# GNN node pass on one core: where the bias of the node product is added

## The chip, the cores and the metric

The kernel runs on one core of a Trainium2 chip. The metric is the device time of one execution in microseconds, the median over runs. A core has five engines that run their own instruction streams and meet at semaphores: TensorE (PE, matrix products into the accumulators), VectorE (DVE), ScalarE (ACT), GpSimd (POOL) and SyncE (SP, which here issues DMAs).

## The reference, cut to what matters

Four graph layers follow each other over 50000 nodes of 128 features and 25000 edges. After each one the input is added and every row is normalised. The change concerns the third layer's end and what is computed from it for the fourth:

```
x2   = output of the second layer, normalised            # 50000 x 128
agg  = edge terms of layer 3, summed per node             # 50000 x 128, from the pass before
sfeat = (x2 @ W + b) / (in_deg + 1)
x3   = layernorm(x2 + agg(+ b) + sfeat)
xt   = x3 @ W4.T + bias4                                  # layer 4's transform
alpha_src, alpha_dst = per-head sums of xt * a_src, xt * a_dst
```

Here b appears twice, once plainly and once divided by in_deg + 1. With rin = 1 / (in_deg + 1), a node's row before normalising is x2 + agg + b + rin * (x2 @ W + b).

## The kernel before

All phases run one after the other in one launch. Most of the time goes to layer 2, whose gathers are issued by GpSimd. The phase of interest is the combined node pass, which computes x3 and xt in one sweep. The nodes lie in 30 chunks (CHUNKS), each of 128 partitions by 13 columns (NJ) by 128 features, and a tail of 80 rows. Three slots (SLOTS) of buffers rotate.

For a chunk c in slot s the work goes through these steps. The semaphore that ends each step is in brackets.

- SP loads x2 into X2L and agg into YL (`load`, d_ld). It does so when the same slot's normalised rows have been stored (`store`).
- GpSimd, in `add` (lines 1927 to 1941): it copies the chunk's 13 values of nsrc into R1 (line 1930), multiplies the broadcast bias B2 by the broadcast R1 into the tile BT (line 1933), adds X2L onto YL (line 1937) and adds BT onto YL (line 1941, d_x2y). nsrc was set to rin + 1 at the head of the phase by VectorE (line 1972), so BT is b * (rin + 1).
- TensorE, in `turn`: it transposes X2L in groups of four columns (line 2106, d_t); ACT copies each group out of the accumulators into HT or OT (line 2036, `turned`, d_tc); TensorE multiplies it by W into one of two accumulator banks, SUM + q % 2 (line 2116, d_z).
- VectorE, in `rows`: per group q, it waits for the product (d_z), and for each column adds rin times the product onto YL (line 2001, scalar_tensor_tensor, d_v1). Then `spread` takes the statistics of the group before (line 1989). After the four groups (4, 4, 4 and 1 columns) come the statistics of the last one and the aggregates to mean and variance (line 2011, d_st).
- GpSimd, in `scale`: (variance + eps) to the power -1/2 and minus the mean times that (lines 743 to 749, d_rdy).
- ACT normalises each column into X3 (line 2042, `applied`, d_x3).
- TensorE, in `transform`: it transposes X3 (line 2127), ACT copies (line 2053), and TensorE multiplies by the fourth layer's matrix (line 2137, d_q) in groups of three columns. VectorE, in `transformed`, adds that layer's bias into O3 (line 2019) and copies the attention part (line 2025); SP stores.

Each engine has a fixed order. GpSimd: scale(c), add(c+2), scale(c+1), and so on. VectorE and TensorE: rows or turn of c+1, then transformed or transform of c. ACT mixes: the copy of group 0 of chunk c+1, the normalising of group 0 of chunk c, the copy of group 1, the normalising of group 1, and so on, and then the transform's copies of chunk c. TensorE may overwrite an accumulator bank only when VectorE's scaled additions from it are done (d_v1).

Of the kernel before, what the change touches and what calls it, by code (L numbers as in the profile page):

```python
# [7 lines left out]
P, D = 128, 128  # L8
# [18 lines left out]
NJ = 13  # L27
CHUNKS = NC_ // NJ
SLOTS = 3
# [6 lines left out]
def build(nc, x0, src, dst, ea, ew, w0, b0, w1, b1, gamma, beta, w2, b2, we, be, coef, linw, linb, asrc, adst, out):  # L36
# [8 lines left out]
    def sem(name):  # L45

        phase.append(nc.alloc_semaphore(name=name))
        return phase[-1]
# [19 lines left out]
    with ctx:  # L68
# [622 lines left out]
        def columns(table, c):  # L691

            return table[0:TAIL, NC_:NCOL] if c is None else table[:, bass.ds(c * NJ, NJ)]
# [955 lines left out]
        at = U * CW  # L1649
# [18 lines left out]
        with nc.Block() as block:  # L1668
# [193 lines left out]
        AC = big[:, at:at + 9].rearrange("p (k b) -> p k b", k=3)  # L1862
        CF = big[:, at + 16:at + 19]
        A3 = big[:, at + 32:at + 35]
        R1 = big[:, at + 40:at + 40 + NJ]
        at += 60
        BT = big[:, at:at + NJ * D].rearrange("p (j f) -> p j f", f=D)
        d_w, d_p, d_m, d_ready, d_r1, d_r1b = (sem("d_" + n) for n in "w p m ready r1 r1b".split())
        d_ld, d_x2y, d_st, d_ps, d_rdy, d_x3, d_o, d_sx, d_so = (sems("dd_" + n, SLOTS) for n in (
            "ld x2y st ps rdy x3 o sx so".split()))  # L1870
        d_t, d_tc, d_z, d_v1, d_u, d_uc, d_q, d_oc = (sem("d_" + n) for n in "t tc z v1 u uc q oc".split())
        TR, UB = (HT, OT), (5, CAR)
        QA, QB = -(-NJ // 4), -(-NJ // 3)

# [9 lines left out]
        with nc.Block() as block:  # L1884
# [38 lines left out]
            @block.gpsimd  # L1923
            def _(pool):
                pool.wait_ge(d_ready, 1)

                def add(c, s, n):
                    np_, nj = size(c)
                    y, b = YL[s][0:np_, 0:nj, :], BT[0:np_, 0:nj, :]
                    nc.gpsimd.tensor_copy(R1[0:np_, 0:nj], columns(nsrc, c)).then_inc(d_r1, 1)  # L1930
                    steady(pool, SLOTS * n + s + 1)
                    pool.wait_ge(d_r1, SLOTS * n + s + 1)
                    nc.gpsimd.tensor_tensor(b, wide(B2, np_, nj), R1[0:np_, 0:nj].unsqueeze(2)
                                            .to_broadcast([np_, nj, D]), ALU.mult).then_inc(d_r1b, 1)
                    steady(pool, 32 * n + 32)
                    pool.wait_ge(d_ld[s], 32 * n + 32)
                    nc.gpsimd.tensor_tensor(y, y, X2L[s][0:np_, 0:nj, 0:D], ALU.add).then_inc(d_x2y[s], 1)
                    steady(pool, SLOTS * n + s + 1, 2 * n + 1)
                    pool.wait_ge(d_r1b, SLOTS * n + s + 1)
                    pool.wait_ge(d_x2y[s], 2 * n + 1)  # L1940
                    nc.gpsimd.tensor_tensor(y, y, b, ALU.add).then_inc(d_x2y[s], 1)

                def scale(c, s, n):
                    ln_scale(pool, c, s, n, d_st, d_ps, d_rdy)
                add(0, 0, 0)
                add(1, 1, 0)
                with pool.Fori(0, CHUNKS // SLOTS - 1) as i:
                    for u in range(SLOTS):
                        scale(SLOTS * i + u, u, i)
                        add(SLOTS * i + u + 2, (u + 2) % SLOTS, i + (u + 2) // SLOTS)  # L1950
                m = CHUNKS // SLOTS - 1
                scale(CHUNKS - 3, 0, m)
                add(CHUNKS - 1, 2, m)
                scale(CHUNKS - 2, 1, m)
                add(None, 0, m + 1)
                scale(CHUNKS - 1, 2, m)
                scale(None, 0, m + 1)

            @block.vector
            def _(dve):  # L1960
# [8 lines left out]
                                                                    ALU.mult, ALU.add))  # L1969
                nc.vector.tensor_scalar(B3C, ones[:], A3[:, 2:3], None, ALU.mult)  # L1970
                nc.vector.tensor_copy(IDA[:, 0:D], ident[:])
                nc.vector.tensor_scalar(nsrc[:], rin[:], 1.0, None, ALU.add)
                link(dve, "dve", nc.vector.memset(IDA[:, D:DX], 0.0))
                for k in range(2):
                    for q in range(HEADS):
# [16 lines left out]
                def rows(c, s, n):  # L1992

                    np_, nj = size(c)
                    steady(dve, 2 * n + 2)
                    dve.wait_ge(d_x2y[s], 2 * n + 2)
                    for q, js in groups(c, 4):
                        dve.wait_ge(d_z, before_chunk(c, QA) + q + 1)
                        for j in js:
                            rc = rin[0:np_, NC_:NCOL] if c is None else rin[:, bass.ds(c * NJ + j, 1)]  # L2000
                            ins = nc.vector.scalar_tensor_tensor(YL[s][0:np_, j, :], PS[0:np_, SUM + q % 2, j % 4, :],
                                                                 rc, YL[s][0:np_, j, :], ALU.mult, ALU.add)
                        ins.then_inc(d_v1, 1)
                        if q:
                            spread(c, s, q - 1, groups(c, 4)[q - 1][1])
                    q, js = groups(c, 4)[-1]
                    spread(c, s, q, js).then_inc(d_st[s], 1)
                    steady(dve, 2 * n + 1)
                    dve.wait_ge(d_st[s], 2 * n + 1)
                    for j in range(nj):  # L2010
                        ins = nc.vector.bn_aggr(mv[0:np_, s, j, :], st6[0:np_, j, :])
                    ins.then_inc(d_st[s], 1)
# [415 lines left out]
```

## Time and profile before

| | |
|---|---|
| median of 3 runs | 9455.91 us (9445.86 to 9458.88) |
| profiled execution | 9455.72 us, span 9453.9 us |
| mean granted TensorE clock | 0.63 |
| GpSimd busy | 6665.9 us (71%) |
| TensorE busy | 5807.2 us (61%) |
| VectorE busy | 4952.6 us (52%) |
| ScalarE busy | 2449.6 us (26%) |

The busy shares are means over phases with different limits. The node pass lies between about 7938 and 8392 us from the span's start, so only what the views show of this stretch bears on the change. In the rows, L numbers are lines of the kernel before; a name such as big stands for many tiles that are cut out of one large buffer (X2L, YL, X3, O3, BT among them), and PS stands for the accumulators.

### The profile page before, as it was taken

The page shows a single profiled execution, that of the slowest core. Times are in us where ns is not written, and L with a number is a line of the kernel's source. Part 1 is how long each engine was busy: PE and PEld are TensorE (multiplying, and loading weights), DVE is VectorE, ACT ScalarE, POOL GpSimd, SP SyncE. Part 2 cuts the span into 40 slices and gives each one's busy share as a digit, 9 for nine tenths or more (in the row PEclk, how much of TensorE's full clock was granted, in tenths as well). Part 3 has the DMA queues.
Part 4 walks back from the last instruction along what each step waited for, and adds up shares of the span by engine and source line. Part 5 has one row for each costly group of instructions (what it writes and reads, how often), then busy time and mean ns, then how long its engine had stood idle before and what let it go on. Part 6 is the DMA issues. An engine that isn't in the chain of part 4 may idle for free. (4 is left out here: it accounts for less than half of the span.)

```text
span 9453.9 us, 109668 instructions
## 1 busy us (share of the span) xinstructions
PE 5807.2 (61%) x24229; PEld 4281.7 (45%) x24229; DVE 4952.6 (52%) x12073; ACT 2449.6 (26%) x6228; POOL 6665.9 (71%) x6509
## 2 busy tenths in 40 slices
PE   4646556777775677765777765777751676730190
PEld 2436223555554555554555544555541565630170
DVE  5669665563334753335743345633347675630277
ACT  0116000222224222224222233222236112630006
POOL 4767674477777777777777777777777677977566
PEclk8765786775555765555855556855555787975555
DMA  3127101566664766654766666666656223631118
GB/s 146 43 89 264 29 2 26 110 119 100 101 104 98 129 111 99 101 100 103 137 102 101 101 100 115 124 101 105 101 100 226 83 67 119 248 125 29 20 32 330
DMA packets 472142, 1025.40 MB, mean 108 GB/s; under 512 B 146139, under 2 KB 179724, under 8 KB 471396
## 3 DMA queue, kind: packets, MB, share of 16 engines
q0 software_dynamic: 192032, 330.70, 29.6%
q1 hardware_dynamic: 262212, 589.56, 17.4%
q10 hardware_dynamic: 17664, 102.61, 2.6%
q8 instruction: 75, 1.23, 0.1%
q14 instruction: 159, 1.30, 0.0%
HBM read 562.28 MB, written 472.47 MB: 109 GB/s over the span
## 5 line engine op out<-in xcount | busy, mean ns | idle before, releaser
L1018 POOL DMA_INDIRECT G<-tab,gidx x4000 | 3960.3, 990 | 1617.0 <-issue 1408.4
L1365 PE MATMUL PS<-M,G 128*128 128x128 f32 x6400 | 2257.8, 476 | 1299.6 <-DMA G<-tab,gidx 902.2
L1365 PEld LDWEIGHTS PS<-M,G 128*128 128x128 f32 x6400 | 1549.4, 311 | 2032.7 <-DMA G<-tab,gidx 1451.9
L1313 ACT ACTIVATE M<-ident,wz 128x128 f32<-128x128 f32 x3200 | 1021.5, 390 | 2376.5 <-DVE UO L1421 1223.8
L1421 DVE TENSOR_TENSOR_SCAN UO<-keyrow,UT,PS 128x512 f32<-128x512 f32 (+1 forms) x400 | 511.8, 1279 | 1290.5 <-PE PS L1365 1290.5
L1421 DVE TENSOR_TENSOR_SCAN UT<-keyrow,UO,PS 128x512 f32<-128x512 f32 (+1 forms) x400 | 511.8, 1279 | 1190.4 <-PE PS L1365 1190.4
L758 ACT ACTIVATE big<-big,nb,rs 128x128 f32<-128x128 f32 x1173 | 461.3, 480 | 426.7 <-POOL nb L749 360.3
L1105 POOL DMA_INDIRECT Y<-pair_d,G x400 | 402.7, 1007 | 199.8 <-issue 130.6
L1443 DVE TENSOR_TENSOR Y<-PS,big 128x512 f32<-128x512 f32 x800 | 535.9, 670 | 14.0 <-PE PS L1390 7.5
L1390 PE MATMUL PS<-ident,UT 128*128 128x128 f32 x1600 | 422.5, 419 | 8.3 <-DVE UT L1421 8.3
L1390 PE MATMUL PS<-ident,UO 128*128 128x128 f32 x1600 | 423.1, 420 | 0.0
L1368 PE MATMUL PS<-ident,G 128*128 128x128 f32 x800 | 189.2, 308 | 358.3 <-DMA G<-tab,gidx 308.0
L1331 ACT ACTIVATE M<-PS,tcol,scol 128x512 f32<-128x512 f32 x200 | 155.5, 778 | 842.2 <-PE PS L1368 842.2
L1257 PE MATMUL PS<-big 128*128 128x400 f32 x800 | 323.6, 531 | 43.2 <-DVE G L1151 25.9
L1390 PEld LDWEIGHTS PS<-ident,UT 128*128 128x128 f32 x1600 | 343.0, 228 | 14.7 <-DVE UT L1421 14.7
L1390 PEld LDWEIGHTS PS<-ident,UO 128*128 128x128 f32 x1600 | 346.1, 229 | 0.0
L2270 PE MATMUL PS<-ident,cf 128*100 128x128 f32 x8 | 2.0, 426 | 517.4 <-DVE cf L2216 517.4
L450 POOL DMA_INDIRECT G<-in_x,ridx x200 | 207.6, 1038 | 157.5 <-DVE ridx L520 95.1
L2314 POOL DMA_INDIRECT agg<-Y,sidx x200 | 197.8, 989 | 153.5 <-DVE Y L2365 105.0
L902 POOL DMA_INDIRECT gidx<-lastpos,src_i x200 | 229.9, 1149 | 102.4 <-issue 67.3
L1368 PEld LDWEIGHTS PS<-ident,G 128*128 128x128 f32 x800 | 108.8, 148 | 418.9 <-DMA G<-tab,gidx 366.3
L1384 PE MATMUL PS<-cf 128*128 128x512 f32 x400 | 261.0, 741 | 14.6 <-DVE UT L1421 7.6
(500 smaller groups left out, 11173.4 us busy)
## 6 DMA issues: line engine op xcount, KB each, us to landing
tab<-Y SPq DMA_DIRECT2D x1050, 256.0 KB, 2.8
big<-agg SPq DMA_DIRECT2D x90, 832.0 KB, 8.2
G<-tab,gidx POOLq DMA_INDIRECT x4000, 3.8
WR<-w_d SPq DMA_DIRECT2D x200, 256.0 KB
big<-x SPq DMA_DIRECT2D x60, 832.0 KB, 4.9
xt_d<-big SPq DMA_DIRECT2D x30, 884.0 KB, 3.6
x2n<-big ACTq DMA_DIRECT2D x30, 838.5 KB, 3.5
big<-x2n SPq DMA_DIRECT2D x30, 838.5 KB, 5.4
```

What stands on the lines that cost most here:

```text
L758: ins = nc.scalar.activation(X[0:np_, j, 0:D], V[0:np_, j, :], ACT.Identity, scale=rs[0:np_, s, j:j + 1], bias=nb[0:np_, s, j:j + 1])
L902: pool.indirect_dma_start(gidx[:, t:t + 1], None, lastpos, bass.IndirectOffsetOnAxis(ap=src_i[:, t:t + 1], axis=0)).then_inc(g_got, 16)
L1018: pool.indirect_dma_start(G[:, t % RG, 0:D], None, tab_in(k), bass.IndirectOffsetOnAxis(ap=gidx[:, t:t + 1], axis=0)).then_inc(l_got[t % R ...
L1105: pool.indirect_dma_start(GS[:, t, :], None, pair_d, bass.IndirectOffsetOnAxis(ap=G2[:, t:t + 1], axis=0)).then_inc(o_got, 16)
L1257: ins = nc.tensor.matmul(bank2(n % 2)[:, j, :], OH[:, 2 * n + j, :], CT, start=True, stop=True)
L1313: ins = nc.scalar.activation(M[:, GR * h + j, :], ident[:], ACT.Copy, scale=wz[:, bass.ds((NB * i + q) * GR + j, 1)])
L1365: ins = nc.tensor.matmul(PS[:, FT_[h], j, :], G[:, s, 0:D], M[:, GR * h + j, :], start=True, stop=True)
L1368: ins = nc.tensor.transpose(PS[:, FT_[h], j, :], G[:, s, 0:D], ident[:])
L1384: nc.tensor.matmul(bank(BK_[h]), QR[:, q % NG, :], BD, start=True, stop=False)
L1390: ins = nc.tensor.transpose(PS[:, BK_[h], j, :], UR[h][:, j, :], ident[:])
L1421: nc.vector.tensor_tensor_scan(S[h], keyrow[:, bass.ds(tile * P, GR * P)], half if k == 0 else bank(FT_[h]), S[1 - h][:, GR * P - 1:GR * P ...
L1443: nc.vector.tensor_tensor(group_of(Y, q % NG), PS[:, BK_[h], :, :], zt_at((NB * i + q) * GR).rearrange("p (s f) -> p s f", f=D), ALU.add). ...
```

## The change

VectorE now adds the broadcast bias to a group's product in the accumulator bank, in place, in one instruction per group of up to four columns, and signals it on a new semaphore d_zb. The scaled additions of the group wait for it; they then add rin * (product + b). The statistics of the group before move to between the bias addition and the wait, so they now come ahead of the group's scaled additions and not behind them. GpSimd no longer copies the column and no longer multiplies; its second addition adds the broadcast bias itself. The column R1, the tile BT, their two semaphores and VectorE's setup instruction for nsrc are gone.

```diff
-                    y, b = YL[s][0:np_, 0:nj, :], BT[0:np_, 0:nj, :]
-                    nc.gpsimd.tensor_copy(R1[0:np_, 0:nj], columns(nsrc, c)).then_inc(d_r1, 1)
-                    steady(pool, SLOTS * n + s + 1)
-                    pool.wait_ge(d_r1, SLOTS * n + s + 1)
-                    nc.gpsimd.tensor_tensor(b, wide(B2, np_, nj), R1[0:np_, 0:nj].unsqueeze(2)
-                                            .to_broadcast([np_, nj, D]), ALU.mult).then_inc(d_r1b, 1)
+                    y = YL[s][0:np_, 0:nj, :]
                     steady(pool, 32 * n + 32)
                     pool.wait_ge(d_ld[s], 32 * n + 32)
                     nc.gpsimd.tensor_tensor(y, y, X2L[s][0:np_, 0:nj, 0:D], ALU.add).then_inc(d_x2y[s], 1)
-                    steady(pool, SLOTS * n + s + 1, 2 * n + 1)
-                    pool.wait_ge(d_r1b, SLOTS * n + s + 1)
+                    steady(pool, 2 * n + 1)
                     pool.wait_ge(d_x2y[s], 2 * n + 1)
-                    nc.gpsimd.tensor_tensor(y, y, b, ALU.add).then_inc(d_x2y[s], 1)
+                    nc.gpsimd.tensor_tensor(y, y, wide(B2, np_, nj), ALU.add).then_inc(d_x2y[s], 1)
...
-                nc.vector.tensor_scalar(nsrc[:], rin[:], 1.0, None, ALU.add)
...
                     for q, js in groups(c, 4):
                         dve.wait_ge(d_z, before_chunk(c, QA) + q + 1)
+                        product = PS[0:np_, SUM + q % 2, 0:len(js), :]
+                        nc.vector.tensor_tensor(product, product, wide(B2, np_, len(js)), ALU.add).then_inc(d_zb, 1)
+                        if q:
+                            spread(c, s, q - 1, groups(c, 4)[q - 1][1])
+                        dve.wait_ge(d_zb, before_chunk(c, QA) + q + 1)
                         for j in js:
                             rc = rin[0:np_, NC_:NCOL] if c is None else rin[:, bass.ds(c * NJ + j, 1)]
                             ins = nc.vector.scalar_tensor_tensor(YL[s][0:np_, j, :], PS[0:np_, SUM + q % 2, j % 4, :],
                                                                  rc, YL[s][0:np_, j, :], ALU.mult, ALU.add)
                         ins.then_inc(d_v1, 1)
-                        if q:
-                            spread(c, s, q - 1, groups(c, 4)[q - 1][1])
```

## Rows read from the trace of the kernel before

**Rows 1.** Windows: stretch, length, each engine's busy time (instructions), clock, DMA share, GB/s.
```profile
7983.64:8363.27 379.63, 293.60 (x2107) 249.62 (x2108) 261.18 (x1215) 240.52 (x595) 362.32 (x216) 0.99 0.63 244
8363.27:8376.62 13.35, 10.10 (x73) 8.32 (x72) 9.67 (x45) 8.55 (x22) 4.42 (x7) 1.00 0.34 135
```

**Rows 2.** Groups by line, 7965 to 8370: busy us, mean ns, then idle before.
```profile
L1941 POOL TENSOR_TENSOR big<-big 128x1664 f32<-128x1664 f32 (+1 forms) x30 | 108.4, 3613 | 5.1 <-POOL big L1937 5.1
...
L1937 POOL TENSOR_TENSOR big<-big 128x1664 f32<-128x1664 f32 (+1 forms) x29 | 96.0, 3311 | 0.0
L1933 POOL TENSOR_TENSOR big<-big 128x1664 f32<-128x1664 f32 (+1 forms) x29 | 84.4, 2910 | 4.2 <-POOL big L1930 0.2
...
L746 POOL TENSOR_TENSOR rs<-rs,minus_half 128x13 f32<-128x13 f32 x29 | 71.2, 2457 | 2.4
```

**Rows 3.** Timeline of an early chunk: start, us, engine, line, count, [idle before, releaser].
```profile
7979.80 1.04 DVE L2019 TENSOR_TENSOR big<-PS,big 128x408 f32<-128x408 f32 x2
7980.04 0.27 POOL L743 TENSOR_SCALAR rs<-mv 128x13 f32<-128x13 f32 x1 [0.37 <-DVE mv L2011]
...
7983.14 0.59 ACT L2036 COPY HT<-PS 128x512 f32<-128x512 f32 x1 [1.30 <-PE PS L2106]
...
7983.64 1.65 ACT L2042 ACTIVATE big<-big,nb,rs 128x128 f32<-128x128 f32 x4
...
7985.08 1.13 DVE L2001 SCALAR_TENSOR_TENSOR big<-PS,rin,big 128x128 f32<-128x128 f32 x4 [1.78 <-PE PS L2116]
7985.20 0.56 ACT L2036 COPY OT<-PS 128x512 f32<-128x512 f32 x1
...
7985.81 1.16 PE L2116 MATMUL PS<-big,OT 128*128 128x128 f32 x8 [0.44 <-ACT OT L2036]
...
7987.12 1.13 DVE L2001 SCALAR_TENSOR_TENSOR big<-PS,rin,big 128x128 f32<-128x128 f32 x4 [0.91 <-PE PS L2116]
...
7989.14 1.13 DVE L2001 SCALAR_TENSOR_TENSOR big<-PS,rin,big 128x128 f32<-128x128 f32 x4
...
7990.18 0.86 DVE L1989 BATCH_NORM_STATS2 st<-big 128x6 f32<-128x128 f32 x4
...
7990.96 0.33 DVE L2001 SCALAR_TENSOR_TENSOR big<-PS,rin,big 128x128 f32<-128x128 f32 x1
...
7992.37 0.97 DVE L2011 BATCH_NORM_AGGREGATE mv<-st 128x2 f32<-128x6 f32 x13
...
7993.26 1.04 DVE L2019 TENSOR_TENSOR big<-PS,big 128x408 f32<-128x408 f32 x2
```

**Rows 4.** Timeline: VectorE reads accumulators in another phase.
```profile
2013.52 0.67 DVE L1426 TENSOR_TENSOR big<-PS,bias 128x512 f32<-128x512 f32 x1
2014.10 0.68 DVE L1443 TENSOR_TENSOR Y<-PS,big 128x512 f32<-128x512 f32 x1
```

**Rows 5.** Groups of VectorE by form, whole run.
```profile
L1421 DVE TENSOR_TENSOR_SCAN UO<-keyrow,UT,PS 128x512 f32<-128x512 f32 x320 | 409.5, 1280 | 929.4 <-PE PS L1365 929.4
...
L342 DVE MEMSET PS<- 128x4096 f32 x1 | 3.5, 3472 | 0.9 <-DVE wccol L341 0.9
```

**Rows 6.** Timeline of the tail's one group on VectorE.
```profile
8376.62 0.35 DVE L2001 SCALAR_TENSOR_TENSOR big<-PS,rin,big 80x128 f32<-80x128 f32 x1 [0.33 <-PE PS L2116]
...
8377.01 0.29 DVE L1989 BATCH_NORM_STATS2 st<-big 80x6 f32<-80x128 f32 x1
8377.40 0.18 DVE L2011 BATCH_NORM_AGGREGATE mv<-st 80x2 f32<-80x6 f32 x1
```

**Rows 7.** Timeline of the pass's start.
```profile
7955.26 2.16 DVE L2001 SCALAR_TENSOR_TENSOR big<-PS,rin,big 128x128 f32<-128x128 f32 x8 [10.84 <-POOL big L1941]
...
7965.62 0.28 POOL L743 TENSOR_SCALAR rs<-mv 128x13 f32<-128x13 f32 x1
...
7969.26 1.65 ACT L2042 ACTIVATE big<-big,nb,rs 128x128 f32<-128x128 f32 x4 [8.78 <-POOL nb L749]
```

**Rows 8.** Waits, 7965 to 8370: us in total, times, longest.
```profile
DVE big L2001 <- PE PS L2116: 97.8, 60, 6.6
```

More of the change, by code:

```diff
@@ L1864, in build @@
         A3 = big[:, at + 32:at + 35]
-        R1 = big[:, at + 40:at + 40 + NJ]
         at += 60
-        BT = big[:, at:at + NJ * D].rearrange("p (j f) -> p j f", f=D)
-        d_w, d_p, d_m, d_ready, d_r1, d_r1b = (sem("d_" + n) for n in "w p m ready r1 r1b".split())
+        d_w, d_p, d_m, d_ready = (sem("d_" + n) for n in "w p m ready".split())
         d_ld, d_x2y, d_st, d_ps, d_rdy, d_x3, d_o, d_sx, d_so = (sems("dd_" + n, SLOTS) for n in (
             "ld x2y st ps rdy x3 o sx so".split()))
-        d_t, d_tc, d_z, d_v1, d_u, d_uc, d_q, d_oc = (sem("d_" + n) for n in "t tc z v1 u uc q oc".split())
+        d_t, d_tc, d_z, d_zb, d_v1, d_u, d_uc, d_q, d_oc = (sem("d_" + n) for n in "t tc z zb v1 u uc q oc".split())
         TR, UB = (HT, OT), (5, CAR)
```

## The prediction

> **What bounds the kernel now.** I read the page first (shares and the slices), then the windows of the node pass, its groups of instructions, its waits, and last the timeline of one chunk. Over the whole run GpSimd is the busiest engine, but most of that is gather issue in other phases. The change is inside the combined node pass alone, some 450 us of the 9454, in 30 chunks of 13 columns and a tail. So the question is what one chunk costs there.
>
> Call a round the time from one chunk's first normalising activation (ACT L2042) to the next chunk's. From chunk 1 to chunk 28 there are 27 rounds in 379.63 us, so 14.06 us each, and GpSimd is busy for 362.32 of them, 13.4 a round [rows 1]. The groups say with what: three passes over 1664 elements, 2.91, 3.31 and 3.61 us on average, and the power for the inverse root, 2.46 [rows 2]. With its small instructions and gaps that is the whole round: GpSimd sets the pace. The TensorE clock was granted at 0.99, its upper level.
>
> But a second ring lies just below. The last full round has almost no GpSimd work (4.42 us busy) and still takes 13.35 us [rows 1]. The timeline of an early chunk shows the ring's members [rows 3]:
> - ACT copies the turned group 0 of the next chunk (7983.14), 0.50 later it starts to normalise group 0 of this chunk (7983.64), 1.56 later it copies turned group 1 (7985.20), 0.61 later TensorE multiplies it by W (7985.81), 1.31 later VectorE's scaled addition of group 1 starts (7987.12).
> - From there VectorE is back to back: group 2 starts 2.02 later (7989.14), group 3 1.82 after that (7990.96), the aggregates 1.41 after that (7992.37), and the additions of the transform 0.89 after that (7993.26).
> - From those additions to the copy of the next chunk's group 0 it is 3.34 (7979.80 to 7983.14), through TensorE's last products and its next transposes.
>
> Sum: 0.50 + 1.56 + 0.61 + 1.31 + 2.02 + 1.82 + 1.41 + 0.89 + 3.34 = 13.46 us. The other way round, through GpSimd, is as long: its scale step starts 0.24 after the transform's additions (7979.80 to 7980.04, the one place where it waited for VectorE, 0.37 us) and the activation comes 3.60 after that; 0.24 + 3.60 = 3.84, just the 3.34 + 0.50 of the other branch. So GpSimd's 14.06 stands over a ring of latencies of 13.46, only 0.6 us less.
>
> **The change part by part.**
>
> *GpSimd's bias product and column go.* Per chunk 2.91 to 3.00 us and a copy with its gap, 3.3 together. GpSimd then needs 14.06 - 3.3 = 10.8 us a round. This alone would give the round to the ring: 13.46. The remaining additions keep their number; the second now reads a broadcast instead of a filled tile. The pass that read broadcasts took 2.91, the one that read two filled tiles 3.61 [rows 2]: 0 to 0.7 us gained, no matter where the round is over 11.
>
> *VectorE adds the bias in the accumulators.* Three additions of 512 elements and one of 128 per chunk. Nothing in the trace adds from an accumulator into an accumulator. The nearest rows read an accumulator and write SBUF: 0.67 us, and the next instruction starts 0.58 later [rows 4]. Bounds from both sides: a fill of all 4096 elements of the accumulators took 3.47 us, so 0.43 for 512 of writing; and the slowest two-input 512-element form on this engine, the scan, took 1.28 [rows 5]. I take 0.60 as the start-to-start price, beside the 0.58, and 0.25 for the 128-element one, a quarter of the 1.04 that four scaled additions take (7989.14 to 7990.18).
>
> The Trainium skill prices this differently: Perfetto Trace Analysis, Optimizing Scalar/DVE Operations, gives VectorE some 125 ns of access per instruction on PSUM, which on top of 512 elements at the 0.96 GHz of VectorE: DVE Perf Modes is an estimate of 0.66 between starts. The row says 0.58; by the page the total below would be some 3 us more.
>
> *Where these stand.* Group 0 is covered. VectorE starts it 5.28 after the transform's additions (7979.80 to 7985.08) [rows 3]; with the addition (0.67), the new wait (0.1) and four scaled additions (1.04) it is done at 7.1, and group 1's product arrives at 3.34 + 3.98 = 7.32. So the idle before group 1 pays for it, with 0.2 to spare. From group 1 on it is not covered, as VectorE has no idle left in the ring:
> - group 1 to 2: 0.60 + four statistics 0.78 (7990.18 to 7990.96) + 1.04 = 2.42 in place of 2.02, so +0.40 (0.20 of the old time was a wait for TensorE, which is absorbed)
> - group 2 to 3: 2.42 in place of 1.82, +0.60
> - group 3 to the aggregates: 0.25 + 0.78 + 0.39 + 0.39 = 1.81 in place of 1.41, +0.40. The two 0.39 are new: the statistics of group 3 now stand right behind the scaled addition they read. The tail shows both steps bare: 8376.62, 8377.01, 8377.40 [rows 6]. Before, group 2's statistics hid the first.
>
> The other new wait, for the bias addition, is hidden for groups 1 to 3 by the statistics of the group before. Queued behind it on VectorE is only the scaled addition itself. TensorE waits for that one before it overwrites an accumulator; group 2's product is wanted 2.02 after group 1's and is ready by then, as the scaled addition of group 0 ends before group 1's begins.
>
> The ring is then 13.46 + 0.40 + 0.60 + 0.40 = 14.86 us, both branches alike, as they part only behind the aggregates. That is 0.80 a round *more* than the 14.06 that GpSimd imposed: the change takes 3.3 us off an engine that was 0.6 over the ring, and puts 1.4 on the ring.
>
> *Loads.* A chunk's tiles are asked for when its slot's normalised rows are stored, and GpSimd will want them some 3 us sooner than now. It has 14.86 - 10.8 = 4 us a round of slack, so even a wait of 3 us there is hidden.
>
> *Start and end.* Now the first scaled addition starts at 7955.26 and waits for GpSimd's three passes; then GpSimd does chunk 1's passes, and scales chunk 0 only at 7965.62, 3.64 before the first activation at 7969.26 [rows 7]. After: the setup loses one column instruction (0.3) and GpSimd 3.1, so VectorE starts near 7951.8. Its chunk takes 1.82 + 2.42 + 2.42 + 1.81, and 1.1 for the aggregates and the signal, 9.6 in all, to 7961.4, where GpSimd is already free. The first activation comes 4.2 earlier. The first round grows by 1.4, as does the last full one, which never waited for GpSimd. The tail's own bias addition runs under the last chunk's 13 activations and costs nothing.
>
> Sum: -4.2 + 1.4 + 27 x 0.80 + 1.4 = +20.2 us. The profiled execution lasted 9455.72 (span 9453.9), and the median shown is 9455.91, so its time stands for the median. Forecast: **9476 us**, +0.21%.
>
> **The rivals.**
> - *The additions fall into VectorE's idle time.* That idle is real: 97.8 us in 60 waits for TensorE's product [rows 8], 3.5 us a round against 2.05 added. If groups 2 and 3 came late enough from ACT and TensorE, the ring would stay at 13.46 and the round would fall by 0.6: 27 x -0.60 - 4.2 = -20, 9436 us. It decides if the idle lies behind group 1. Against it: of the idle 0.91 to 1.78 us at a time stands ahead of group 0 and of group 1 [rows 3], and only 0.2 behind. Chance 0.11.
> - *Writing accumulators is dear.* At 0.9 us start to start, groups 1 and 2 cost 0.3 each more, group 3 0.1, and group 0 outgrows its cover by 0.1: a round of 15.7, 27 x 1.6 + 2 x 2.2 - 3 = +45, 9500 us. At the scan's 1.2 it would be near 9528. For it: no row shows this form. Against it: the fill writes 512 in 0.43. Chance 0.16.
> - *Half of it is absorbed.* Between the ring and the rounds there may be slack that I took for fixed: were only 0.7 of the 1.4 to show, the round would be 14.16 and the total 27 x 0.1 - 4 + 1 = 0, 9456 us. This would happen if ACT, whose next copies follow its own queue, gave group 1 sooner. Against it: 13.35 and 13.46 in two rounds of different kinds. Chance 0.12.
> - *The forecast,* with the start-to-start price between 0.55 and 0.67 and 0.1 of error in the small steps: 9468 to 9485. Chance 0.61.
>
> **How the numbers follow.** What a measurement of this kernel can tell from no change is some 0.2%, 19 us, so slower begins at 9475, inside the forecast's own range. I split its 0.61 into 0.34 above and 0.27 below. Slower: 0.34 + 0.16 = 0.50. Same: 0.27 + 0.12 = 0.39. Faster: 0.11. The range for 8 in 10 reaches from the half-absorbed case to the dear accumulators: 9454 to 9500.
>
> **What the changed profile would show.** Right: rounds of ACT L2042 near 14.9; GpSimd busy near 10.3 a round, with idle before its scale step released by VectorE's aggregates; an idle before group 0 and group 1 only, the second near 0.2; a bias addition near 0.67 with the next start 0.6 later; the first activation near 7965. Wrong: rounds of 13.5, or idle between the bias addition of group 2 and its scaled addition; a bias addition well over 0.7 us; a GpSimd that still never waits; a TensorE clock that falls in the pass.

## The result and the profile after

The changed kernel takes 9468.03 us (median of 20 runs, 9459.94 to 9480.95), the kernel before 9450.84 in as many. The ratio is 1.0018, with a 95% interval of 1.0011 to 1.0025: slower by about 17 us. The forecast was 9476, +20.2 on its own base. Two executions of the kernels below stood far out (12583.7 us of e1_gp_alone, 10008.3 of e6_pe_bias_copies_first); they don't count in the ratios.

The profiled execution after lasted 9470.05 us, span 9468.1; the clock is as before (0.63), TensorE and ScalarE are so within 0.3%, VectorE has 64 us more, GpSimd 99 us less. In the page's first part (busy us, share, instructions):

```profile
PE 5791.9 (61%) x24229; PEld 4293.8 (45%) x24229; DVE 5016.2 (53%) x12193; ACT 2446.4 (26%) x6228; POOL 6566.6 (69%) x6447
```

Phases in which nothing was changed differ between executions: this pass begins 6.4 us earlier than in the profile before, and over all profiles below its start varies by 21 us. So below I measure the pass itself, in the one profiled execution of each kernel. VectorE writes a one-element note ahead of the pass and behind it, and the timeline of these gives the length of the pass after:

```profile
7925.40 0.06 DVE L170 MEMSET note<- 1x1 f32 x1 [16.81 <-PEq L52]
8405.29 0.06 DVE L170 MEMSET note<- 1x1 f32 x1
```

That is 479.89 us. Between the same two notes the kernel before takes 463.34 (7931.78 to 8395.12). So the pass is 16.55 longer, which accounts for the difference of the medians, 17.19. The windows of the pass after, as those of [rows 1], hold the 27 rounds and the last full one:

```profile
7973.84:8371.19 397.35, 286.34 (x2106) 245.35 (x2106) 317.53 (x1323) 237.59 (x595) 278.73 (x163) 1.00 0.60 234
8371.19:8385.84 14.65, 10.18 (x73) 8.53 (x73) 11.76 (x49) 8.54 (x24) 3.83 (x6) 1.00 0.31 123
```

A round is now 14.72 us on average in place of 14.06 and the last one 14.65 in place of 13.35. GpSimd is busy for 10.3 us of a round, no longer 13.4. The waits of the two engines within the 27 rounds (total us, count, longest) say who waits now:

```profile
POOL rs L743 <- DVE mv L2005: 101.6, 27, 4.1
...
DVE PS L1991 <- PE PS L2110: 47.1, 27, 1.9
```

GpSimd waits 3.8 us a round for VectorE's aggregates, where before all its waits for them came to 0.7 us in 27 rounds. VectorE waits 1.7 us for TensorE once a round, ahead of group 0; ahead of group 1 some 0.15 is left (below), and behind it none. The groups of instructions of the pass give the price of the new operation (lines renumbered: L1991 is the bias addition, L1997 the scaled addition):

```profile
L1991 DVE TENSOR_TENSOR PS<-PS,big 128x512 f32<-128x512 f32 x90 | 62.7, 696 | 63.8 <-PE PS L2110 55.0 <-POOL big L1933 7.5
...
L1991 DVE TENSOR_TENSOR PS<-PS,big 128x128 f32<-128x128 f32 x30 | 8.7, 290 | 0.0
```

And the timeline of one early chunk, the counterpart of [rows 3]:

```profile
7970.01 1.04 DVE L2013 TENSOR_TENSOR big<-PS,big 128x408 f32<-128x408 f32 x2
...
7970.25 0.27 POOL L743 TENSOR_SCALAR rs<-mv 128x13 f32<-128x13 f32 x1 [4.90 <-DVE mv L2005]
...
7973.35 0.58 ACT L2030 COPY HT<-PS 128x512 f32<-128x512 f32 x1 [1.30 <-PE PS L2100]
...
7973.84 1.65 ACT L2036 ACTIVATE big<-big,nb,rs 128x128 f32<-128x128 f32 x4
...
7975.18 0.70 DVE L1991 TENSOR_TENSOR PS<-PS,big 128x512 f32<-128x512 f32 x1 [1.67 <-PE PS L2110]
7975.40 0.56 ACT L2030 COPY OT<-PS 128x512 f32<-128x512 f32 x1
...
7976.01 1.16 PE L2110 MATMUL PS<-big,OT 128*128 128x128 f32 x8 [0.43 <-ACT OT L2030]
7976.02 1.13 DVE L1997 SCALAR_TENSOR_TENSOR big<-PS,rin,big 128x128 f32<-128x128 f32 x4
7977.21 0.70 DVE L1991 TENSOR_TENSOR PS<-PS,big 128x512 f32<-128x512 f32 x1
7977.81 0.86 DVE L1980 BATCH_NORM_STATS2 st<-big 128x6 f32<-128x128 f32 x4
7978.59 1.11 DVE L1997 SCALAR_TENSOR_TENSOR big<-PS,rin,big 128x128 f32<-128x128 f32 x4
7979.62 0.69 DVE L1991 TENSOR_TENSOR PS<-PS,big 128x512 f32<-128x512 f32 x1
...
7982.02 0.29 DVE L1991 TENSOR_TENSOR PS<-PS,big 128x128 f32<-128x128 f32 x1
...
7983.77 0.97 DVE L2005 BATCH_NORM_AGGREGATE mv<-st 128x2 f32<-128x6 f32 x13
7984.65 1.04 DVE L2013 TENSOR_TENSOR big<-PS,big 128x408 f32<-128x408 f32 x2
...
7988.00 0.58 ACT L2030 COPY HT<-PS 128x512 f32<-128x512 f32 x1 [1.30 <-PE PS L2100]
7988.48 1.65 ACT L2036 ACTIVATE big<-big,nb,rs 128x128 f32<-128x128 f32 x4
```

Walk the ring from 7973.35: 0.49 to the activation, 1.56 to the copy of group 1, 0.61 to its product and 1.20 to its bias addition (7977.21). VectorE then steps through 7979.62, 7982.02, 7983.77 and 7984.65, that is 2.41, 2.40, 1.75 and 0.88, and it is 3.35 to the next copy. Together 14.65. It is the ring of the prediction, with VectorE back to back from group 1's addition on. Ahead of that addition stand 1.19 us for group 0's four scaled additions (7976.02 to 7977.21), which take 1.03 where nothing is waited for (7978.59 to 7979.62): the difference, 0.16, is the wait for group 1's product.

### The profile page after: what moved, and what is told of

The parts are those of the page before. It is cut to its first block and busy times, and to the rows that moved or that the text cites. A ratio compares the mean times of both kernels' runs of the same rounds, so it can differ in the third digit from the quotient of the medians.

```text
span 9468.1 us, 109641 instructions
## 1 busy us (share of the span) xinstructions
PE 5791.9 (61%) x24229; PEld 4293.8 (45%) x24229; DVE 5016.2 (53%) x12193; ACT 2446.4 (26%) x6228; POOL 6566.6 (69%) x6447
```

## The experiments

The theory: before, GpSimd's 14.06 a round stood 0.6 over a ring of latencies of 13.46; the change takes GpSimd off the path and puts three new steps of VectorE on the ring, from group 1 on. The rivals: the work taken off GpSimd gives nothing, the additions fall into idle time, or the cost is in the moved statistics rather than in the additions. Each kernel ran 5 to 11 times beside the kernel before on the same chip. First all results; "pass" is the time between the two notes of VectorE in the profiled execution, and the kernel before has 463.34 in it. A round is from one chunk's first activation to the next one's; where two figures stand, the second, 0.23 to 0.32 longer, is every third round.

| kernel | median us | ratio to before | 95% interval | pass us | against before | round us |
|---|---|---|---|---|---|---|
| after | 9468.03 | 1.0018 | 1.0011 to 1.0025 | 479.89 | +16.55 | 14.64 / 14.88 |
| e1_gp_alone | 9423.57 | 0.9979 | 0.9970 to 0.9989 | 443.04 | -20.30 | 13.45 / 13.69 |
| e2_dve_alone | 9467.67 | 1.0028 | 1.0018 to 1.0037 | 483.87 | +20.53 | 14.65 / 14.88 |
| e3_old_order | 9503.94 | 1.0065 | 1.0051 to 1.0079 | 523.40 | +60.06 | mostly 16.0 to 16.7 |
| e4_group0_only | 9431.18 | 0.9986 | 0.9977 to 0.9995 | 443.00 | -20.34 | 13.45 / 13.69 |
| e5_pe_bias | 9448.93 | 0.9992 | 0.9983 to 1.0001 | 455.52 | -7.82 | 13.45 / 13.77 |
| e6_pe_bias_copies_first | 9452.54 | 0.9998 | 0.9989 to 1.0007 | 459.20 | -4.14 | 12.76, 13.96, 14.25 |
| e7_old_order_pe_busy | 9492.96 | 1.0043 | 1.0029 to 1.0057 | 500.29 | +36.95 | 15.31 / 15.54 |
| e8_no_power | 9471.63 | 1.0019 | 1.0009 to 1.0028 | 476.81 | +13.47 | 14.64 / 14.87 |
| e9_pe_bias_early_split | 9425.23 | 0.9983 | 0.9974 to 0.9992 | 443.67 | -19.67 | 13.45 / 13.77 |
| e10_pe_bias_copies_first_busy | 9403.89 | 0.9958 | 0.9944 to 0.9971 | 423.76 | -39.58 | 12.76 / 13.08 |
| e11_after_copies_first | 9454.21 | 1.0014 | 1.0005 to 1.0023 | 472.73 | +9.39 | 14.50 / 14.74 |

The medians of the kernel before beside them were 9442.27 (e1 to e4), 9455.21 (e5 to e8) and 9442.68 (e9 to e11). The differences of the medians agree with those of the pass to within 5 us, but for e4_group0_only: its median is 11.1 us under the kernel before and its pass 20.3. All differences of the pass lie within the 95% intervals.

**The two halves of the change.** First GpSimd's half alone, from the changed kernel (it leaves out the bias over in_deg + 1, so its result differs):

```diff
-                        nc.vector.tensor_tensor(product, product, wide(B2, np_, len(js)), ALU.add).then_inc(d_zb, 1)
-                        if q:
-                            spread(c, s, q - 1, groups(c, 4)[q - 1][1])
-                        dve.wait_ge(d_zb, before_chunk(c, QA) + q + 1)
...
+                        if q:
+                            spread(c, s, q - 1, groups(c, 4)[q - 1][1])
```

> GpSimd's part of the change alone: no column copy, no multiplication, VectorE without the bias addition and with its old order (the share of the bias divided by in_deg + 1 is left out of the result). Ring theory: GpSimd was 0.6 us a round over a ring of latencies of 13.46 us, so of its 3.3 us a round only 0.6 shows: rounds of 13.4 to 13.5, 27 x -0.6 and some -5 to -6 at the start, -20 to -22 us in all. Rival, GpSimd as the true bound of the pass: rounds of 10.8, -90 us. Rival, VectorE's waits absorb nothing and something else holds the rounds at 14: -5 us.

Measured: rounds of 13.45, the ring's length, as the timeline of ACT shows (a third round of 13.69, then one of 13.45):

```profile
8107.03 1.65 ACT L2033 ACTIVATE big<-big,nb,rs 128x128 f32<-128x128 f32 x4
...
8120.72 1.65 ACT L2033 ACTIVATE big<-big,nb,rs 128x128 f32<-128x128 f32 x4
...
8134.17 1.65 ACT L2033 ACTIVATE big<-big,nb,rs 128x128 f32<-128x128 f32 x4
```

So taking GpSimd's product away does give something, 20.30 us, of which 14.4 are in the 27 rounds and 6.1 ahead of the first activation, and no more than the ring below allows. Then VectorE's half alone, from the kernel before, with GpSimd's copy and product kept in its queue and only not read by its last addition:

```diff
-                    nc.gpsimd.tensor_tensor(y, y, b, ALU.add).then_inc(d_x2y[s], 1)
+                    nc.gpsimd.tensor_tensor(y, y, wide(B2, np_, nj), ALU.add).then_inc(d_x2y[s], 1)
...
+                        nc.vector.tensor_tensor(product, product, wide(B2, np_, len(js)), ALU.add).then_inc(d_zb, 1)
```

> VectorE's part alone: bias addition in the accumulators and the moved statistics, while GpSimd still copies the column and multiplies (its product is computed and not used; it adds the broadcast bias as in the changed kernel). Ring theory: GpSimd's 14.0 us of work fits inside a ring of 14.65, so the rounds are as long as in the changed kernel (14.7) and only the start's gain of 4.6 us is missing: +21 to +22 us against before, some 4 us above the changed kernel. Rival, the multiplication still counts a round (shared ports, or GpSimd still on the path): rounds of 15.2 or more, +35 us.

Measured: the rounds are those of the changed kernel to 0.01 us. Under a ring of 14.65 GpSimd's three passes fit, so their removal is worth nothing in a round. This pass is 3.98 us longer than the changed one's: the first activation, which follows GpSimd's first chunk, comes 4.70 later (37.57 into the pass against 32.87), and the tail is 0.82 shorter (18.63 against 19.45).

**Which additions cost.** The first half again, with the addition to group 0 alone (the share of the other groups is left out):

```diff
+                        if q == 0:
+                            product = PS[0:np_, SUM + q % 2, 0:len(js), :]
+                            nc.vector.tensor_tensor(product, product, wide(B2, np_, len(js)), ALU.add).then_inc(d_zb, 1)
+                            dve.wait_ge(d_zb, (CHUNKS if c is None else c) + 1)
```

> As the first kernel of this call, but VectorE adds the bias in the accumulators for group 0 alone (left out for groups 1 to 3), with its bare wait. Ring theory: group 0 stands in the idle ahead of group 1, so its 0.84 us a round costs nothing: the same time as GpSimd's part alone, within 2 us, about -20 against before. Rival, VectorE's time counts wherever it stands: 28 x 0.84 = +23 over GpSimd's part alone, so about +2 against before.

Measured: 443.00 in the pass against 443.04 without it. In its timeline the scaled additions of group 0 follow 0.84 behind the addition, and those of group 1 another 1.28 on:

```profile
8102.38 0.70 DVE L1992 TENSOR_TENSOR PS<-PS,big 128x512 f32<-128x512 f32 x1 [1.67 <-PE PS L2111]
8103.22 1.13 DVE L1996 SCALAR_TENSOR_TENSOR big<-PS,rin,big 128x128 f32<-128x128 f32 x4
8104.50 1.13 DVE L1996 SCALAR_TENSOR_TENSOR big<-PS,rin,big 128x128 f32<-128x128 f32 x4
```

Four of them take 1.03 from start to start (7978.59 to 7979.62 above, with no gap), so about 0.2 of the cover was left. In these two passes group 0's addition is free, and the whole cost is that of groups 1 to 3. The medians say it less sharply: this kernel's is 7.6 us above that of the first half. The added time that the rival named (+2 against before, ratio 1.0002) lies outside this kernel's interval, but no trace was kept of an execution at its median, so where the 7.6 us lie is open.

**What the moved statistics do.** The changed kernel, with the statistics back behind the scaled additions:

```diff
-                        if q:
-                            spread(c, s, q - 1, groups(c, 4)[q - 1][1])
                         dve.wait_ge(d_zb, before_chunk(c, QA) + q + 1)
...
                         ins.then_inc(d_v1, 1)
+                        if q:
+                            spread(c, s, q - 1, groups(c, 4)[q - 1][1])
```

> The changed kernel with the statistics put back behind the scaled additions, so that VectorE waits bare for each bias addition. Ring theory: bias addition 0.70 + 0.14 wait in place of 0.60 start to start, for groups 1 and 2 each +0.25, group 3 +0.09: rounds of 15.2 to 15.3, +33 us against before (+16 against the changed kernel). Rival, the wait is cheap and the order does not matter: +17 as the changed kernel.

Measured: 523.40, 43.5 more than the changed kernel and far more than a bare wait can cost (0.84 from the addition's start to its reader's, against 0.60 to an independent instruction). The timeline shows an addition's bare wait, and then something else:

```profile
8112.86 0.68 DVE L1991 TENSOR_TENSOR PS<-PS,big 128x512 f32<-128x512 f32 x1
...
8113.69 1.13 DVE L1995 SCALAR_TENSOR_TENSOR big<-PS,rin,big 128x128 f32<-128x128 f32 x4
...
8118.95 1.70 PE L2131 MATMUL PS<-big,UO 128*128 128x136 f32 x6 [2.39 <-DVE big L2013]
...
8120.65 1.53 PE L2131 MATMUL PS<-big,UT 128*128 128x136 f32 x6
```

Six products with 136 columns, 0.96 us for the same shape earlier in the chunk, take 1.70 after TensorE has stood idle for 2.39. The windows around the idle time give the granted clock in the third column from the end:

```profile
8112.90:8118.90 6.00, 3.41 (x26) 2.84 (x26) 5.61 (x32) 1.98 (x5) 1.13 (x3) 0.98 0.81 305
8118.90:8120.50 1.60, 1.55 (x7) 1.58 (x8) 0.39 (x1) 0.00 (x0) 1.52 (x2) 0.50 1.00 412
```

It fell from 0.98 to 0.50, the lower of its two levels (1.2 GHz), and those products are on the ring. To tell that from the order itself, the same kernel with products whose result nobody reads, into an accumulator that is free, ahead of the wait in which TensorE stood idle, in the chunks of the loop:

```diff
+                        if q == 2 and not isinstance(g, int):
+                            for j in range(12):
+                                nc.tensor.matmul(PS[:, PA, j % 4, :], W2, ident[:], start=True, stop=True)
```

> The kernel with the statistics in the old order (e3_old_order), and TensorE does 12 products of 128 columns into free accumulators ahead of its long wait for VectorE in the transform (their result is never read). In e3_old_order some rounds took 15.26 us, as worked out, and most 16.2 to 16.7, with TensorE's products at 1.5 to 1.7 us in place of 0.94 after 2.4 us of idle. Clock theory: TensorE without the long idle keeps its upper level, all rounds are 15.3, +33 to +37 us against before. Rival, the long rounds come from the order itself or from memory: +60 us or more, as the fillers only add work.

Measured: rounds of 15.31, the best rounds of the one before (15.26), and a granted clock of 1.00 over 300 us in place of 0.92. Windows of the two kernels, old order first:

```profile
8000.00:8300.00 300.00, 215.92 (x1434) 188.72 (x1433) 220.86 (x913) 160.33 (x400) 186.64 (x111) 0.92 0.56 218
```

```profile
8000.00:8300.00 300.00, 257.81 (x2001) 230.09 (x2000) 233.82 (x964) 169.36 (x423) 198.44 (x118) 1.00 0.59 230
```

So at least 23.1 of the 43.5 us were the clock; the last chunks, outside the loop, have no such products, and one of their rounds still takes 16.39. The rounds in the loop stay 0.66 us above the changed kernel's. The bare waits account for it by the sum made ahead of the run (+0.25, +0.25 and +0.09 for groups 1 to 3, 0.59), which no run splits further. The place of the statistics, which I had only counted as cover, saves more (43.5 us) than the additions cost in it (479.89 - 443.04 = 36.85).

**Both branches.** The changed kernel without GpSimd's power, 2.45 us of its branch of the ring. The call is replaced by its own instructions, without the power that stood between the second and the third:

```diff
-                    ln_scale(pool, c, s, n, d_st, d_ps, d_rdy)
...
+                    nc.gpsimd.tensor_scalar(rs[0:np_, s, 0:nj], mv[0:np_, s, 0:nj, 1], EPS, None, ALU.add)
+                    nc.gpsimd.tensor_scalar(nb[0:np_, s, 0:nj], mv[0:np_, s, 0:nj, 0], -1.0, None,
+                                            ALU.mult).then_inc(d_ps[s], 2)
...
+                    nc.gpsimd.tensor_tensor(nb[0:np_, s, 0:nj], nb[0:np_, s, 0:nj], rs[0:np_, s, 0:nj],
+                                            ALU.mult).then_inc(d_rdy[s], 1)
```

> The changed kernel without the power in GpSimd's scale step (the rows are scaled by variance + eps instead of its inverse root, so the result differs), 2.46 us less between the aggregates and ScalarE. By the prediction both branches of the ring are alike, through GpSimd's scale step and through the transform and the copy of group 0, and ScalarE does the copy first: rounds stay at 14.65 to 14.75, +16 to +18 us against before, the first activation 2.5 us earlier and the last one too. Rival, the ring closes through GpSimd alone: rounds of 12.2, -50 us.

Measured: the rounds stay at 14.64; only the ends lose 3.1 us. So the ring's other branch, through TensorE's transposes and ACT's copy, holds the ring by itself, and GpSimd's branch was no longer than it.

**Moving the bias to TensorE.** The first half alone leaves TensorE with idle time. Here a product of ones with the bias row, split into three bf16 parts, starts each accumulation, while TensorE waits for ACT's copy:

```diff
+                        nc.tensor.matmul(PS[0:np_, SUM + q % 2, 0:len(js), :], ONB[:, 0:np_], wide(BB, P, len(js)),
+                                         start=True, stop=False, skip_group_check=True)
+                        pe.wait_ge(d_tc, g + 1)
...
-                                                   start=True, stop=True)
+                                                   start=False, stop=True, skip_group_check=True)
```

> TensorE adds the bias: ahead of its wait for ScalarE's copy it starts each accumulator group with one single-pass bf16 product of a matrix of ones with the bias split into three bf16 rows (their sum is the fp32 bias), and the products by W accumulate onto it. VectorE has no bias addition and its old order, GpSimd no multiplication. Ring theory: four short products a chunk fall into TensorE's idle time ahead of each product (0.24 to 0.75 us), nothing is added to the ring: rounds of 13.4 to 13.5 with 13.7 in every third, -18 to -22 us against before, level with GpSimd's part alone. Rival, TensorE is the next bound and each start of a group delays the product by its own 0.2 to 0.4: rounds of 14 and more, -5 us or nothing.

Measured: the rounds are 13.45, so the bias costs a round nothing there. But the pass is 12.5 longer than the bare first half, and not level with it as expected. Of this 11.4 lie ahead of the first activation (42.71 us into the pass against 31.35), where VectorE splits the bias row, and 0.9 in the tail:

```profile
7924.31 3.38 POOL L1934 TENSOR_TENSOR big<-big 128x1664 f32<-128x1664 f32 x1 [23.36 <-DVE big L1977]
7924.47 3.31 DVE L1981 CAST big<-big 128x128 bf16<-128x128 f32 x1
...
7927.84 3.82 POOL L1937 TENSOR_TENSOR big<-big 128x1664 f32<-128x1664 f32 x1
7928.14 3.60 DVE L1983 CAST big<-big 128x128 bf16<-128x128 f32 x1
7931.77 3.37 DVE L1984 TENSOR_TENSOR big<-big 128x128 f32<-128x128 f32 x1
7935.17 3.74 DVE L1985 CAST big<-big 128x128 bf16<-128x128 f32 x1
```

Instructions on 128 elements take as long as GpSimd's additions of 1664 beside them. Its first subtraction, by chance between two of GpSimd's additions, took 0.29. The next kernel has the same split earlier, while GpSimd is still idle:

```diff
                 nc.vector.tensor_copy(col[:, 6:7], ones[:, 0:1]).then_inc(d_p, 1)
+                nc.vector.memset(ONB, 1.0)
...
+                ins.then_inc(d_bb, 1)
                 dve.wait_ge(d_m, 1)
```

> e5_pe_bias with the split of the bias into bf16 rows moved ahead of the point where GpSimd starts its additions. In e5_pe_bias the rounds were 13.45 us as worked out, but the pass was only 7.8 us shorter than before and not 20: VectorE's four instructions of the split that touch GpSimd's port each took 3.3 to 3.7 us, as long as GpSimd's addition beside them, and TensorE's first transposes waited for them. Port theory: alone on VectorE they take 0.2 to 0.3 us each, mostly inside the 1.45 us in which VectorE waits for TensorE, so the pass is 19 to 21 us shorter than before, -18 to -22 us. Rival: these instructions are slow by themselves (conversion to bf16), and the loss of 12 us stays: -8 us.

```profile
7933.39 0.16 DVE L1977 CAST big<-big 128x128 bf16<-128x128 f32 x1
7933.59 0.29 DVE L1978 TENSOR_TENSOR big<-big 128x128 f32<-128x128 f32 x1
7933.91 0.23 DVE L1979 CAST big<-big 128x128 bf16<-128x128 f32 x1
```

The same instructions take 0.16 to 0.29, the first activation comes at 31.44, the pass is 443.67, and the gain of the first half is kept with the full computation done: 0.9983.

**Shortening the ring.** ACT copies the turned groups 0 and 1 before it normalises, so that group 1's product no longer waits for four activations:

```diff
-                        if k < len(first):
-                            turned(ahead, *first[k])
+                        if k == 0:
+                            for f in first[0:2]:
+                                turned(ahead, *f)
+                        elif k + 1 < len(first):
+                            turned(ahead, *first[k + 1])
```

On top of TensorE's bias (with the late split):

> As the run before it in this call, and ScalarE copies group 1 of the next chunk ahead of the first normalising group of this one, so that the first normalising group (1.56 us) leaves the ring. Ring theory: what is left is VectorE from group 0 on, 5.28 + 1.04 + 1.04 + 0.78 + 1.04 + 0.78 + 0.25 + 1.16 + 0.89 = 12.26, and the chain over the normalised rows and the transform at 12.3 to 12.9: rounds of 12.3 to 12.9, -40 to -50 us against before. Rival, the 13.46 is set by something else than this ring (loads, TensorE): rounds stay at 13.5, -20 us.

Measured: one round in three is 12.76, as worked out, but the others are 13.96 and 14.25, and most of the gain is lost. In a long round TensorE's transposes and products come behind 1.45 us of idle time and take 1.40 and 1.73, in a short one 0.88 and 0.96; the granted clock is 0.57 over these 4 us of the long round and 1.00 over the same steps of the short one. The timeline of a long one, then of a short one:

```profile
8119.39 1.40 PE L2138 MATMUL PS<-ident,big 128*128 128x128 f32 x6 [1.45 <-ACT big L2047]
...
8120.71 1.73 PE L2148 MATMUL PS<-big,UO 128*128 128x136 f32 x6
...
8133.62 0.88 PE L2138 MATMUL PS<-ident,big 128*128 128x128 f32 x6 [1.45 <-ACT big L2047]
...
8134.74 0.96 PE L2148 MATMUL PS<-big,UO 128*128 128x136 f32 x6 [0.24 <-ACT UO L2058]
```

The same edit with the early split, and four unread products into a free accumulator ahead of the wait in which TensorE stood idle:

```diff
+                        for j in range(4):
+                            nc.tensor.matmul(PS[:, PA, j, :], W2, ident[:], start=True, stop=True)
```

> e6_pe_bias_copies_first with the early split, and with four products of 128 columns on TensorE into free accumulators (never read) ahead of its wait for the normalised rows. In e6_pe_bias_copies_first one round in three took 12.76 us, inside the 12.3 to 12.9 worked out, and two 13.96 and 14.25, with TensorE's transposes and products at 1.4 and 1.73 in place of 0.88 and 0.96 behind an idle of 1.45 us, the granted clock at 0.92 over 300 us in place of 1.00. Clock theory: with the idle filled, all rounds take 12.8, 13.0 in every third: 27 x -1.2 and -5 at the start, -35 to -42 us against before. Rival: the longer rounds come from GpSimd's waits for the loads (2 us a round): rounds of 13.5 to 14 stay, -15 us.

Measured: 12.76 and 13.08 in all rounds, 423.76 in the pass, 9403.89 us. Windows of the kernel without the products and of the one with them:

```profile
8000.00:8300.00 300.00, 261.89 (x1807) 230.06 (x1806) 213.19 (x987) 194.84 (x485) 226.34 (x130) 0.92 0.66 255
```

```profile
8000.00:8300.00 300.00, 277.52 (x2102) 243.43 (x2103) 223.18 (x1042) 205.59 (x514) 239.74 (x141) 1.00 0.70 274
```

The clock went from 0.92 to 1.00. The early split doesn't explain the rounds: without ACT's edit they were 13.45 with the late and with the early one. This version beats both kernels: 0.9958 against the kernel before (0.9944 to 0.9971), 38.8 us. And the changed kernel itself with ACT's edit alone:

> The changed kernel with ScalarE's copy of group 1 ahead of its first normalising group, and nothing else. Ring theory: the slack that the prediction gave group 0 (0.2 us) is all there is before VectorE alone sets the round: from the transform's additions 5.2 to group 0, 0.84 + 1.04 for it, then 2.41 + 2.40 + 1.75 + 0.88 = 14.5, in place of 14.65: -4 us against the changed kernel, +13 against before. If TensorE now idles longer ahead of the normalised rows its clock may fall as in e6_pe_bias_copies_first, and rounds of 15.5 to 16 stand beside them. Rival: the first normalising group is still what holds the ring, and rounds fall by its 1.56 us: 13.1, -30 us.

Measured: 14.50 in place of 14.65. With group 1's product no longer late, VectorE is back to back from group 0 on; its wait ahead of group 1 was 0.15 us, which is all that the same edit gives a round here, against 0.7 where VectorE has no additions. The pass is 7.16 shorter than the changed kernel's: 3.9 of this are in the 27 rounds, the rest at the two ends (the tail is 18.31 in place of 19.45).

## Why the prediction held

By its steps, each against the pass:

| step | predicted | measured |
|---|---|---|
| start to the first activation | -4.2 | -4.61 (37.48 to 32.87) |
| first round | +1.4 | +1.19 (14.38 to 15.57) |
| 27 rounds | +21.6 | +17.72 (379.63 to 397.35) |
| last full round | +1.4 | +1.30 (13.35 to 14.65) |
| tail | 0 | +0.95 (18.50 to 19.45) |
| sum | +20.2 | +16.55 |

- *GpSimd stands 0.6 over a ring of 13.46.* Shown by its half alone: 13.45.
- *Group 0 is covered, with 0.2 to spare.* Shown by the kernel with group 0 alone, within 0.04 us of the pass without.
- *GpSimd's removal is worth nothing under the new ring, and about 4 at the start.* Shown by VectorE's half alone: same rounds, 4.70 at the start. The other branch of the ring is no longer than the first: shown by the kernel without the power.
- *The price of an addition.* Predicted 0.60 from start to start, by the row of an addition that reads accumulators and writes SBUF [rows 4]. Measured 0.60 (7977.21 to 7977.81), and a busy time of 0.696. The Trainium skill's access time (Perfetto Trace Analysis, Optimizing Scalar/DVE Operations) made an estimate of 0.66; the measurement decides for 0.60.
- *The mis-sized term: 27 rounds at +0.80.* They cost 17.72 / 27 = 0.66 each. The ring is 14.65, not 14.86. Of this difference of 0.21, 0.11 is the step from the product's start to VectorE, now 1.20 where the scaled addition came 1.31 behind it [rows 3], and 0.10 the steps on VectorE (2.41, 2.40, 1.75, 0.88 against 2.42, 2.42, 1.81, 0.89). Most of the latter is group 3, whose two steps I took bare from the tail [rows 6]. Against that I left something out: every third round is 0.24 longer. It shows in the after kernel and in every kernel whose rounds are set by the ring, once per body of the loop of three slots; eight of the 27 rounds have it, which is 2.0 us. In the trace it stands as an idle time of 0.22 of TensorE's weight loading, ahead of a chunk's first transposes, with nothing that the profile shows to wait for. The kernel before has the same idle time (0.21), and its longer round hid it, so I could have read it only from that row. That the turn of the loop is its cause is my reading and was not tried.
- *The tail at nothing.* It measures 0.95 more, but that is not the price of the change. In every kernel TensorE begins the last transform at the lower clock, after idling under the last chunk's 13 activations, and what differs is how soon the clock comes back. The second six products with 136 columns took 0.92 before and 1.57 after; in VectorE's half alone, which has the same additions in its tail, they took 1.06:

```profile
8385.41 0.92 PE L2137 MATMUL PS<-big,UT 128*128 128x136 f32 x6
```

```profile
8394.62 1.57 PE L2131 MATMUL PS<-big,UT 128*128 128x136 f32 x6
```

```profile
8407.01 1.06 PE L2140 MATMUL PS<-big,UT 128*128 128x136 f32 x6
```

  The tail is 18.63 in that kernel and 18.31 in e11_after_copies_first, which also has the additions, against 18.50 before; and it is 19.70 in e5_pe_bias and 18.58 in e9_pe_bias_early_split, which differ only in where the bias row is split. So the additions in the tail cost nothing, as predicted. Why the clock came back late in six of the twelve changed kernels (after, e5, e6, e7, e8, e10) is open.

The forecast's 9476 was 8 us too high: 5 of these are its base, the median of 3 runs where 20 gave 9450.84, and 3 are the sum. That the sum came so near is in part luck: the ring's 0.21 a round is 5.7 us too much in 27 rounds, and against it stand 2.0 for the third rounds, which it didn't have, and the tail's 0.95.

Of the rivals, none came: VectorE's idle time lies ahead of groups 0 and 1 and not behind them; accumulator writes are not dear; half of the added time was not absorbed. What the prediction named as a sign of error, a TensorE clock that falls in the pass, did not appear in the rounds of the change (granted 1.00), but in those of its neighbours: that the loss is no larger, the change owes to the moved statistics.

## What to carry to other kernels

Before work is moved off the busiest engine, add up the ring of latencies below it: that ring, not the work removed, sets the gain, and an engine that is back to back on that ring is the worst place to move the work to. Look for an engine that waits at the right moment (here TensorE, waiting for ACT's copy, takes the bias with rounds still at 13.45), and put independent work between an operation and its reader on the same engine. When an edit makes TensorE wait a little longer, read the granted clock of the rounds before reading the edit's price.

## What the runs showed of the hardware

- TensorE's granted clock fell to its lower level behind idle times of 2.39 us in the old order and 1.45 us in the copies-first kernel, and cost 1.2 us in a round of the latter (12.76 to 13.96, and 13.08 to 14.25 where the round is a third one). It did not fall behind 1.45 us in that kernel's short rounds, nor in the changed kernel, which idles 1.79 us (below). So the length of one idle time alone doesn't tell. Unread products in the idle time brought it back to 1.00 in both cases, over 300 us of the pass. The line of the changed kernel:

```profile
7985.35 0.94 PE L2131 MATMUL PS<-big,UO 128*128 128x136 f32 x6 [1.79 <-DVE big L2013]
```

- VectorE's conversions to bf16 and an addition with both inputs in SBUF ended only with GpSimd's addition beside them: 3.31 to 3.74 us against 0.16 to 0.29 for the same instructions with GpSimd idle. The Trainium skill, SBUF — State Buffer, Who interferes with whom, says that a VectorE instruction with two SBUF inputs, or a copy or cast in its two-port mode, contends with GpSimd for a shared port pair, and that whoever holds it blocks the other; the trace agrees, with these numbers, though no row shows in which mode the casts ran. VectorE's scaled and bias additions, which read accumulators, ran beside GpSimd at their usual 0.34 and 0.70.
- VectorE adds onto an accumulator in place at nearly the price of an addition that reads accumulators and writes SBUF: 0.696 us, the next start 0.60 later, against 0.67 and 0.58 [rows 4]. A reader of the result on the same engine starts 0.84 after it.
- GpSimd's second addition did not get cheaper with a broadcast for its second input: 3.73 us on average in the 27 rounds of the changed kernel, and 3.72 with two filled tiles in those of the kernel before. The mean of 3.61 in [rows 2] has the tail's short one in it.
